# Queries and keys turned by VectorE in 32 by 32 blocks; the last output product moved into the last stage

## The reference

```
# layer 1, condition: attention of 32 query heads and 8 key heads of 128,
# 512 cached keys (16 pages of 32) and 32 new ones for each sequence
q = _rope(_rmsnorm(x @ Wq.T, q_norm_w), pos);  k = _rope(_rmsnorm(x @ Wk.T, k_norm_w), pos);  v = x @ Wv.T
k_all = concat([k_cache[block_table], k]);     v_all = concat([v_cache[block_table], v])
scores = einsum('bqhd,bkhd->bhqk', q, repeat(k_all, 4)) * SCALE   # masked beyond cache_seqlens
o = einsum('bhqk,bkhd->bqhd', softmax(scores), repeat(v_all, 4))
y = o.reshape(bsz, seqlen, HQ * D) @ Wo
# layer 1, feed-forward: y @ W_up.T plus one of 4 low-rank experts, chosen by argmax
# layer 2: 512x512 product with a low-rank adapter for each sequence; then a gated
#          feed-forward (1376 wide) whose matrices are 4 copies of a tile plus rank 2
# layer 3: product with a top-2 mixture of low-rank experts; then an int8 product
```

## Time and profile before

| | |
|---|---|
| median of three runs | 3090.23 us (3088.97 to 3091.32) |
| profiled execution, its own time | 3083.84 us |
| its span; granted clock of TensorE, mean | 3082.1 us; 0.99 |
| busy: TensorE | 2957.8 us (96%) |
| busy: VectorE, ScalarE, GpSimd | 1513.4 (49%), 1240.8 (40%), 1466.0 (48%) |
| transpositions of queries and keys, L359 | 620 records |
| gathers of values, L288 | 504, 971 ns each |

### The profile page before, as it was taken

The page is one execution under the profiler, slowest core; times in us unless marked ns, Lnnn a source line. Parts: engine busy times, 40 slices in busy tenths (PEclk is TensorE's granted clock), DMA queues, the critical chain, the costliest instruction groups (busy, mean ns, idle before and its releaser), DMA issues. The chain is left out here.

```text
span 3082.1 us, 55162 instructions
## 1 busy us (share of the span) xinstructions
PE 2957.8 (96%) x14880; PEld 1968.9 (64%) x14880; DVE 1513.4 (49%) x4171; ACT 1240.8 (40%) x2633; POOL 1466.0 (48%) x1262
## 2 busy tenths in 40 slices
PE   5889999999999999999999999999999998899997
PEld 4566666666666666666666666666666675555664
DVE  4544444444444444444444444444444444576665
ACT  2444444444444444444444444444444442222222
POOL 5555555555555555555555555555555561000000
PEclk9999999999999999999999999999999999999999
DMA  8544443444444444545444434444444444221110
GB/s 308 177 119 121 121 120 119 120 121 121 121 121 121 121 121 121 202 121 175 121 121 121 121 121 121 121 121 121 121 121 121 121 127 147 82 59 35 42 41 14
DMA packets 432363, 369.03 MB, mean 120 GB/s; under 512 B 89558, under 2 KB 370282, under 8 KB 431162
## 3 DMA queue, kind: packets, MB, share of 16 engines
q1 hardware_dynamic: 376922, 186.83, 21.4%
q0 software_dynamic: 48208, 165.16, 16.5%
q10 hardware_dynamic: 7056, 14.46, 1.3%
HBM read 335.13 MB, written 22.71 MB: 116 GB/s over the span
## 5 line engine op out<-in xcount | busy, mean ns | idle before, releaser
L558 DVE CUSTOM_DVE_ANT_0 ps_s<-ps_s,mask 128x544 f32<-128x544 f32 x512 | 374.8, 732 | 932.4 <-PE ps_s L388 813.8
L288 POOL DMA_INDIRECT v_sb<-in_v_rows_w,v_row x504 | 489.1, 971 | 456.2 <-PE ps_oT L416 246.2
L463 ACT ACTIVATE ps_s<-ps_s,nmax 128x544 f32<-128x544 f32 x512 | 352.3, 688 | 875.4 <-DVE nmax L558 791.3
L347 PE MATMUL ps_t<-wqkv,xT 128*128 128x512 f32 x1488 | 700.7, 593 | 0.0
L411 PEld LDWEIGHTS ps_oT<-pT,v_sb 128*128 128x128 f32 x4096 | 528.7, 192 | 188.5 <-issue 175.0
L411 PE MATMUL ps_oT<-pT,v_sb 128*128 128x128 f32 x4096 | 544.1, 276 | 10.2 <-DMA v_sb<-in_v_rows_w,v_row 9.8
L371 PE MATMUL ps_t<-wo,oT 128*128 128x512 f32 x1024 | 521.8, 594 | 1.5 <-ACT oT L477 1.2
L387 PE MATMUL ps_s<-k_sb,qT 128*128 128x416 f32 x1024 | 447.8, 519 | 19.0 <-issue 11.8
L569 DVE TENSOR_SCALAR p_sb<-ps_s,rinv 128x512 f32<-128x512 f32 x512 | 384.4, 751 | 26.9 <-DVE rinv L566 0.3
L396 PEld LDWEIGHTS ps_pT<-ident_sb,p_sb 128*128 128x128 f32 x2048 | 251.6, 141 | 187.8 <-issue 170.0
L347 PEld LDWEIGHTS ps_t<-wqkv,xT 128*128 128x128 f32 x1488 | 254.4, 191 | 178.1 <-issue 178.1
(11 more groups left out here) (226 smaller groups left out, 3281.8 us busy)
## 6 DMA issues: line engine op xcount, KB each, us to landing
k_sb<-in_kT SPq DMA_DIRECT2D x2048, 64.0 KB
v_sb<-in_v_rows_w,v_row POOLq DMA_INDIRECT x512
wo<-in_wo_w POOLq DMA_DIRECT2D x2, 4096.0 KB, 14.1
v_new<-v_raw SPq DMA_DIRECT2D x512, 16.0 KB, 1.8
y_scratch<-y_sb SPq DMA_DIRECT2D x32, 256.0 KB
xT<-x1T_scratch POOLq DMA_DIRECT2D x31, 256.0 KB, 4.5
wqkv<-in_wqkv_w ACTq DMA_DIRECT2D x6, 1024.0 KB, 24.3
wqkv<-in_wqkv_w POOLq DMA_DIRECT2D x6, 1024.0 KB, 13.0
```

Of the source, the lines that this page charges most:

```text
L288: e.indirect_dma_start(out=v_sb[:, b % 2, c, :], out_offset=None, in_=A["v_rows_w"], in_offset=bass.IndirectOffsetOnAxis(ap=v_row[:, b, c: ...
L347: m = e.matmul(ps_t[bank_of(t)][:, :], xT[:, k, :], wqkv[:, k, 512 * t:512 * t + 512], start=k == 0, stop=k == KC - 1)
L463: e.activation(scores(u), scores(u), ACT.Exp, bias=nmax[:, u % 2:u % 2 + 1], scale=-1.0, accum_out=rsum[:, u % 2:u % 2 + 1]).then_inc(expe ...
L558: e.tensor_tensor_reduce(out=scores(u), in0=scores(u), in1=mask[:, b % 2, :], scale=-SCALE, scalar=3e38, op0=ALU.add, op1=ALU.min, accum_o ...
```

## The change

TensorE's `turn_q` and ScalarE's `copy_q` go. VectorE turns the queries and keys in blocks of 32 by 32, straight from `rot` to `qT` and `kT_new`: for each sequence four blocks of keys (32 partitions, 4 heads x 32) and four of queries (16 heads x 32). The layout of `qT` changes accordingly. A table says how many of the 32 blocks stand in each unit of VectorE ahead of the normalisation and behind it. Waits follow: a sequence's first score waits for all eight of its blocks, `place` for the four key ones, and GpSimd's L111 for all 32 of the round before. Round 0 is turned by TensorE in the embedding stage as before.

```
-    TURN_AT = {8: 0, 9: 1, 10: 2, 11: 3, 12: 4}
+    TURN_AT = {11: (2, 2), 12: (1, 1), 13: (1, 1), 14: (2, 2), 15: (1, 1), 0: (2, 2), 1: (2, 2), 2: (2, 2), 3: (3, 3)}
+    LAST_OUT_AT = {u: (2 * u - 4, 2 * u - 2) for u in range(2, 2 + HQH // 2)}
...
+            def turn(r, i, m):
+                b, j = divmod(m, TURNS)
+                rows, at = slice(S * b, S * b + S), slice(S * (j % 4), S * (j % 4) + S)
+                if m == 0:
+                    e.wait_ge(rope_step, STEPS * (r + 1))
+                    wait(e, scored, UNITS * (r - 1))
+                if j == 0:
+                    e.wait_ge(placed, GB * (r - 1) + b + 1)
+                if j < TURNS // 2:
+                    e.transpose(kT_new[at, :, rows], rot[rows, HQH:HT, at]).then_inc(q_turned, 1)
+                else:
+                    e.transpose(qT[at, i, b, :, :], rot[rows, 0:HQH, at]).then_inc(q_turned, 1)
...
+                    turns(r, i, u, 0)
                     if ahead(r, u, 2) is not None:
                         norm(*ahead(r, u, 2))
+                    turns(r, i, u, 1)
```

```
                 if h == 0:
+                    if first(r):
+                        e.wait_ge(q_copied, NQT)
+                    else:
+                        e.wait_ge(q_turned, blocks_turned(r, b))
                     e.wait_ge(dma_k[b % 2], 16 * NPP * (2 * r + b // 2 + 1))
```

The projection weights of the second half keep their six transfers, but they have one semaphore, and the first projection of round 16 waits for all six:

```
-                    if is_(r, GROUPS):
-                        e.wait_ge(dma_wqkv[1][t], 16)
+                    if is_(r, GROUPS) and t == 0:
+                        e.wait_ge(dma_wqkv, 16 * NT)
```

In the last round the output product of round 30 takes two heads in each of units 2 to 9 instead of one in each unit, and its copy follows in unit 10. The last round's own output product leaves the attention stage. Its input `o_last` lies in the room of `wqkv`, and the tail's TensorE runs it around the first transpositions:

```
+            out_product(0, 11)
             e.wait_ge(dma_beside, 16 * len(BESIDE))
             e.wait_ge(padded, 1)
             for p in both:
                 turn_a(0, p)
+            out_product(11, HQH)
             for p in both:
                 gate_logits(0, p)
                 up(0, p)
```

ScalarE copies its result in the tail and SP stores it behind the loads of the first two row tiles. The tail's weights leave SP's queue for GpSimd's: seven of them at the tail's start or, where they lie in the room of `wo`, behind the output product. VectorE's order at the tail's start changes:

```
+            split(b1x, b1s)
             sum_halves(0)
-            split(b1x, b1s)
+            split(b3x, b3s)
+            e.wait_ge(dma_w, 16 * len(AT_ONCE))
+            e.tensor_copy(langf[:, :], langi[:, :]).then_inc(setup, 1)
+            e.tensor_copy(qwb[:], q8[:].rearrange("p k n -> p (k n)").bitcast(I8).rearrange("p (k n) -> p k n", k=KC)).then_inc(setup, 1)
             route(0)
-            split(b3x, b3s)
             for p in both:
                 second(0, p)
-            e.wait_ge(dma_w, REST)
...
```

More of the change, by code:

```diff
@@ L108, in rotate @@
         if not (isinstance(r, int) and r == 0):
-            e.wait_ge(W.q_turned, NQT * r)
+            e.wait_ge(W.q_turned, blocks_turned(r - 1, GB - 1) if not (isinstance(r, int) and r == 1) else NQT)
     for a, m, t in ROPE_PARTS[i]:
@@ L255, in _ @@
             body(ROUNDS - 1, 1, GROUPS - 1)
[L256 to L259, removed]
+            e.wait_ge(y_copied, ROUNDS - 1)
+            e.dma_start(y_d[ROUNDS - 2, :, :], y_sb[:, :]).then_inc(dma_y, 16)
+            e.wait_ge(dma_y, 16 * (ROUNDS - 1))
         @block.gpsimd
@@ L349, in project @@
                     m.then_inc(projected, 1)
[L351 to L360, removed]
             def out_product(r, i, h0, h1):
@@ L482, in copy_y, with place @@
                 e.activation(y_sb[:, :], ps_t[0][:, :], ACT.Copy).then_inc(y_copied, 1)
[L484 to L489, removed]
-                else:
[L491 to L498, removed]
+            def place(r, b):
+                if first(r):
+                    e.wait_ge(q_copied, NQT)
+                else:
+                    e.wait_ge(q_turned, keys_turned(r, b))
                 wait(e, scored, UNITS * r + HKH * (b - 1))
@@ L509, in body @@
                             copy_y(r - 2)
+                    if last(r) and u == 2 + HQH // 2:
+                        copy_y(r - 1)
                     if 1 <= u <= NT and not last(r):
@@ L584, in table, with turns, body @@
                 make_tables(e, W, csn[:, 0, :], csn[:, 1, :])
-            def body(r):
+            def turn(r, i, m):
[10 more added lines that the diff above has]
+                    e.transpose(qT[at, i, b, :, :], rot[rows, 0:HQH, at]).then_inc(q_turned, 1)
+            def turns(r, i, u, part):
+                if u not in TURN_AT or first(r) and u < 11 or last(r) and u >= 11:
+                    return
+                units = range(11, u) if u >= 11 else range(u)
+                m = (0 if u >= 11 else TURN_NEXT) + sum(sum(TURN_AT[v]) for v in units) + part * TURN_AT[u][0]
+                for n in range(m, m + TURN_AT[u][part]):
+                    turn(r + 1 if u >= 11 else r, 1 - i if u >= 11 else i, n)
+            def body(r, i):
                 for u in range(UNITS):
@@ L605, in _ @@
                 mask_next(0, u)
-            rounds(e, body)
+            pairs(e, body)
 MAGIC = 12582912.0
@@ L1040, in inside, with tail @@
     return views
-def tail(nc, sb, pb, sem, there, wo, dma_beside, A, x1_d, y_d, out_d, ident):
+def tail(nc, sb, pb, sem, there, wo, o_last, dma_beside, A, x1_d, y_d, out_d, ident):
     w = {}
@@ L1131, in tail @@
     setup, passed, padded = sem("c_setup"), sem("c_passed"), sem("c_padded")
-    REST = 16 * (len(loads) - 1)
+    AFTER_OUT = [n for n in loads if n in after]
+    AT_ONCE = [n for n in loads if n not in after and n != "idx2"]
+    dma_after, o_done, o_copied = sem("c_dma_after"), sem("c_o_done"), sem("c_o_copied")
     chain = sem("c_chain")
@@ L1171, in _ @@
                 load(0, p)
[L1172 to L1175, removed]
+            e.sem_inc(stored[0], 16)
+            e.wait_ge(o_copied, 1)
+            e.dma_start(y_d[ROUNDS - 1, :, :], outb[1][:, :]).then_inc(stored[1], 16)
             def store(k, p):
@@ L1207, in _, with out_product @@
                 e.wait_ge(stored[p], 16 * (I_STEPS + 1))
+        @block.gpsimd
+        def _(e):
+            for n in AT_ONCE:
+                e.dma_start(w[n][:], A["c_" + n]).then_inc(dma_w, 16)
+            e.wait_ge(o_done, 1)
+            for n in AFTER_OUT:
+                e.dma_start(w[n], A["c_" + n]).then_inc(dma_after, 16)
         @block.tensor
         def _(e):
+            def out_product(h0, h1):
+                for h in range(h0, h1):
+                    m = e.matmul(bank[1][3][:, :], o_last[:, h, :], wo[:, h, :], start=h == 0, stop=h == HQH - 1)
+                if h1 == HQH:
+                    m.then_inc(o_done, 1)
             def turn4(k, p, src, ready, done, id_=ident, to=None):
@@ L1299, in down @@
             def down(k, more):
+                if first(k):
+                    e.wait_ge(dma_w, 16 * len(AT_ONCE))
+                    e.wait_ge(dma_after, 16 * len(AFTER_OUT))
                 for p in both:
```

67 lines of the change are left out of this document (32 added, 35 removed).

## The result

Nine runs of each kernel: 3088.95 us before, 3101.40 after (3096.02 to 3107.58); the ratio is 1.0042, with a 95% interval from 1.0033 to 1.0051. So the change costs 0.42%, 12 to 13 us. Predicted was 3092 with a range from 3058 to 3128, and no measurable change; the prediction's own limit for that was 0.2%, 6.2 us, and the loss is beyond it. The profiled execution of the changed kernel took 3100.82 us (span 3098.6), 16.5 us longer in span than the one before.

| stretch | before | after | difference | predicted |
|---|---|---|---|---|
| start to first rotation | 70.2 | 72.6 | +2.4 | 0 |
| first rotation to the last round | 2452.1 | 2484.9 | +32.8 | +26 |
| last round, to the end of L416 / L415 | 52.3 | 58.2 | +5.9 | +5 |
| from there to the first feed-forward product | 64.0 | 38.8 | -25.2 | -29 |
| rest | 443.5 | 444.0 | +0.5 | 0 |

A forecast was written before the change was run, and what follows sets the result against it. Two equal paths, TensorE's work and GpSimd's rotation and gathers, were taken to bound each round. -3 + 28 + 1 + 5 - 29 = +2 on 3083.84 gave 3086, as a median of runs 3092; range 3058 to 3128.

The forecast's parts named there:

- Two paths of equal length: At unit 12's product: TensorE's own work, 43.65 us from L98, and GpSimd's chain, 43.5 to 44.5, both end.
- The wait of unit 14: TensorE's score for the next round's first sequence waits for VectorE's last query block: 0.9 us a round, +28 us.
- the dear blocks: Rival, slower: from about 1.05 us a query block, longer waits and a late GpSimd chain, +42, 3132 us; chance 0.22.
- The shared port: Rival, slower: query blocks hold GpSimd beside L103, its chain growing up to 2.5 us a round, 3169 us; chance 0.06.
- the cheap wait: Rival, faster: a block of 0.45 us makes unit 14's wait 0.55 us, +17 for +28, 3078 us; chance 0.20.
- -3: Rounds: TensorE's removed transpositions, 68 us, return as waits for gathers at unit 12; only 0.1 us a round is gained.
- rounds of 77.5: Sign that the prediction is right: the length of a round in the changed kernel, in us.
- A wait of about 2 us in each round: Sign that the prediction is right: TensorE waits at L411 in unit 12 of each round.
- The weights' wait before round 16: Second half's first projection waits for all six weight tiles instead of one: +1 us (0 to 5).
- The last round: Four to six more blocks in units 0 to 3 lengthen VectorE's chain, two heads a unit cover part: +5 us.
- The tail: Last unit to first feed-forward product: output product among the loads, 34.0 us from the tail's start, -29 us.
- The other blocks at nothing: Blocks of units 11, 12, 14 and 0 to 3 cost nothing, lying in VectorE's waits or ahead of later needs.

The follow-up runs named there:

- the kernel of the last stage alone: The changed kernel with queries and keys turned on TensorE as before, the last-stage changes kept: 3065.95 us, ratio 0.9928 to the kernel before.

## Why the prediction was right

**Two paths of equal length: right, and shown.** The prediction put the return of TensorE's 68 us at the product of unit 12. It stands there as 70.8 us of waits, where 9.8 were before; a kernel that only lightens TensorE gains nothing, and the best of those that also shorten GpSimd's chain gains the work.

**The wait of unit 14: right in place and size.** 0.9 us a round was predicted, 1.04 measured, 27 us in all by its removal. The query block takes 702 ns for 0.65 to 0.70 assumed, the key block 302 for 0.3, so the dear blocks fall. The shared port falls for the blocks too: GpSimd's L115, which was L103, takes 2.75 us beside three of them, and took 2.75 before, in all 32 rounds of both kernels. (In the rivals' sums the cheap wait is a slip: by the prediction's own steps a block of 0.45 us makes it 0.63 us, not 0.55, and one of 1.05 makes it 1.23, not 1.3.)

**What was missing in the rounds: the clock.** The sum was +26 (-3, +28 and +1) where 32.8 came out. The sign "rounds of 77.5" was 76.6, one of the shortest, plus 0.9; the mean before was 77.3, and 78.2 would have been the sign to look for (78.3 measured). A wait of about 2 us in each round was forecast, but not that the clock may fall behind it: the prediction put that at nothing. Behind six of them it did; those rounds are 0.5 to 1.7 us longer on the way from GpSimd's copy to the next rotation than the usual 34.3, 8 us together. That may also be why the runs spread wider (3096 to 3108), which no run shows. (The Trainium skill, TensorE: Matmul & The Clock Gate, "Part 1: The HAM clock gate", ties the clock to TensorE's activity; the rows agree in that every such stretch follows a wait, but in most rounds the same wait is without one, and no run here tells what decides it: that stays open.) Against that, more was given back than -3: the idle 11.8 us that TensorE had ahead of scores (L387, in ten rounds, at the branch of the loop) are 2.2 after (L386). That they now lie within the wait of unit 14 is inferred; the sum bears it out, 31 for the wait and 8 for the clock less 10 against the 28 us by which the stretches from copy to rotation grew. The weights' wait before round 16 cost 0.7 us from that unit's score to the next (10.9 against 10.2), 1 predicted; in the kernel of the last stage alone the same stretch took 12.2.

**The last round: right in sum by luck.** 5.9 for +5, but I gave 3.9 to the blocks and 0.8 to the heads in pairs. They cost 2.8 and 3.1.

**The tail: 25.2 for 29.** The step that was mis-sized is its start: "about 1 us after the last unit" is 3.0 (the row with PEq L220), and the first eleven heads take 11.2 us and not 9.6, with a granted clock of 0.61 over their first 4 us. Gate and up are 8.8 for 8.8. The other 2.4 us ahead of the first rotation are no finding: the instructions there hardly changed, and in the eleven profiles of this document the first rotation starts anywhere from 70.0 to 72.6.

**The other blocks at nothing: right here, not everywhere.** The last block of unit 3 ends at 1559.10, 4.55 us behind L110 (4.2 predicted), ahead of L123 at 1560.32. But as soon as the waits are gone, the blocks of units 11 to 13 set the round, by up to 1.6 us.

**What the range covered.** The misses in the rounds, the last round and the tail all went the same way and add up to 11.5 us; with the 2.4 at the start the profiled execution is 14 us above the sum, the median 9 above the forecast. The range of 70 us held that easily. The claim of no measurable change did not hold: the tail pays for most of the loss in the rounds, not for all of it.

## What to carry to other kernels

Before work is taken from an engine that looks full, look for a second chain that ends at one of its instructions without a wait: an instruction whose operand arrived only just before it starts. Compare the lengths of both ways to it. Of two chains of the same length, shortening one is worth nothing: 51 us less of TensorE's work gave none, and once GpSimd's chain was shorter too, 59 us came off. Work moved to an engine with room must stand where its result isn't the next thing that the full engine waits for; moving two blocks by one unit was worth 27 us.

## What the runs showed of the hardware

A block turn of 32 partitions by 512 elements of float32 takes 702 ns on VectorE, one of 128 elements 302 ns (means of 496 each). In a row each costs its whole length: three of 512 elements take 2.18 us, two 1.44.

Next to it, something else was stretched. VectorE's next mask (a tensor_scalar from SBUF to SBUF) took 0.50 us before and takes 1.22 where it now stands behind three blocks, beside GpSimd's L115 (from 1557.31, 2.75 us), and ends 0.3 us after that does. It is so in 30 places (1.13 to 1.23 us), all beside L115:

```profile
1556.92 2.18 DVE L584 STREAM_TRANSPOSE qT<-rot 32x512 f32<-32x512 f32 x3
1559.14 1.22 DVE L525 TENSOR_SCALAR mask<-iota_sb,seqf 128x544 bf16<-128x544 f32 x1
```

```profile
1557.31 2.75 POOL L115 TENSOR_TENSOR raw<-raw,rstd 128x1536 f32<-128x1536 f32 x1 [0.17 <-POOL rstd L112]
```

The turns ran beside the same GpSimd instruction at their usual 0.70 (60 turns of 512 elements lie wholly within L115, 0.70 to 0.71 us each). Not every GpSimd instruction stretches the mask: in 31 places it lies wholly within L112, on 128x8 elements, and takes its usual 0.50. (The Trainium skill, SBUF — State Buffer, "Who interferes with whom", lists tensor_scalar among the VectorE instructions that may need the port shared with GpSimd and then wait for it; the row agrees for the mask beside L115, not beside L112, and by the rows the transposition isn't one of them.) Off the path here, it would count where a mask is the next thing waited for.
